# Order of the first loads and of the last products in a convolution and sign-matrix kernel

## The reference

```python
y = conv1d(x, weight, groups=4, K=9, pad=4) + (cond @ c_weight.T)[:, :, None] + bias
w = kernel.astype(float) * 2 - 1          # 1024 x 1024, every entry +1 or -1
out = x + scale * (y @ w)                 # along the 1024 positions
```

## Time and profile before

| | us |
|---|---|
| median of 3 runs | 175.43 (174.07 to 176.49) |
| the profiled execution | 174.09 |
| its span, first to last instruction | 172.2 |
| TensorE matmul busy | 164.2 (95%) |
| VectorE busy | 136.9 (79%) |
| ScalarE busy | 71.8 (42%) |
| GpSimd busy | 37.6 (22%) |
| mean granted TensorE clock | 0.990 |

### The profile page before, as it was taken

One profiled execution on the slowest core, in us unless ns is written; L12 is line 12 of the kernel. 1 busy time (PEld: TensorE's weight loads), 2 busy tenths in 40 slices (PEclk: granted clock), 3 DMA queues, 4 the chain that ended last, 5 costly groups with the idle time before them and its releaser, 6 DMA issues.

```text
span 172.2 us, 2765 instructions
## 1 busy us (share of the span) xinstructions
PE 164.2 (95%) x914; PEld 136.6 (79%) x914; DVE 136.9 (79%) x180; ACT 71.8 (42%) x68; POOL 37.6 (22%) x43
## 2 busy tenths in 40 slices
PE   7699999999999999999999999999999999999791
PEld 2378888998888779887998889887988899888580
DVE  4735493996999999779986899779977997699461
ACT  3201996470791148521781069304842340214000
POOL 4230600005040334006400343043400540000000
PEclk9969999999999999999999999999999999999999
DMA  5688697777799877887977888988888666414006
GB/s 205 139 159 248 249 196 196 125 200 188 143 337 237 256 153 306 184 229 189 297 185 176 262 173 306 225 249 112 331 214 204 94 249 138 105 49 199 0 0 244
DMA packets 27486, 33.38 MB, mean 194 GB/s; under 512 B 3537, under 2 KB 19857, under 8 KB 27473
## 3 DMA queue, kind: packets, MB, share of 16 engines
q1 hardware_dynamic: 22176, 25.63, 54.6%
q10 hardware_dynamic: 4912, 6.78, 14.8%
q0 software_dynamic: 384, 0.81, 2.2%
HBM read 10.06 MB, written 8.40 MB: 107 GB/s over the span
## 4 chain that ended last, share of the span: by engine, by line
PE 92%; DMA 3%; DVE 2%; issue 1%; ACTq 1%; DVEq 0%
PE ps_A L828 30%; PE ps_conv L809 18%; PE ps_C L828 15%; PE ps_conv L786 9%; PE ps_B L828 8%; DMA taps_nat<-weight 3%; PE ps_B L845 2%; PE ps_C L845 2%; PE ps_toep L845 2%; PE ps_A L845 2%; PE ps_toep L828 1%; PE ps_toep L765 1%; PE ps_C L776 1%; PE ps_A L753 1%; DVE sums L250 1%
## 5 line engine op out<-in xcount | busy, mean ns | idle before, releaser
L485 ACT CAST hi<-sums 128x1024 fp32r<-128x1024 f32 x14 | 14.7, 1049 | 44.5 <-DVE sums L622 38.4
L401 POOL TENSOR_TENSOR set<-x_blk 128x512 f32<-128x512 f32 x12 | 17.3, 1461 | 69.7 <-DMA x_blk<-x_phase 69.7
L643 DVE SCALAR_TENSOR_TENSOR x_nat<-ps_A,scale_col,x_nat 128x512 f32<-128x512 f32 x27 | 20.2, 748 | 15.0 <-PE ps_A L828 14.2
L442 ACT COPY x_phase<-x_nat 128x1032 f32<-128x1032 f32 x13 | 27.2, 2135 | 2.2 <-DMA x_nat<-x 2.2
L828 PE MATMUL ps_A<-sign_T,hi 128*128 128x512 f32 x80 | 22.4, 401 | 0.9 <-DVE x_nat L643 0.9
L485 ACT CAST hi<-y_sum 128x1024 fp32r<-128x1024 f32 (+1 forms) x14 | 11.7, 834 | 25.8 <-DMA y_sum<-y_two 16.5
L828 PE MATMUL ps_A<-sign_T,lo 128*128 128x512 f32 x80 | 22.0, 396 | 0.0
L828 PEld LDWEIGHTS ps_A<-sign_T,lo 128*128 128x128 f32 x80 | 15.0, 188 | 3.8 <-DVE lo L632 0.3
L828 PEld LDWEIGHTS ps_A<-sign_T,hi 128*128 128x128 f32 x80 | 14.5, 189 | 4.2 <-issue 1.3
L809 PE MATMUL ps_conv<-toeplitz,w_bytes 128*128 128x128 f32 x144 | 17.2, 276 | 0.4 <-DVE y_two L596 0.4
L809 PEld LDWEIGHTS ps_conv<-toeplitz,set 128*128 128x128 f32 x144 | 16.9, 192 | 0.8 <-issue 0.4
(11 more groups left out here) (108 smaller groups left out, 234.6 us busy)
## 6 DMA issues: line engine op xcount, KB each, us to landing
x_nat<-x SPq DMA_DIRECT2D x16, 512.0 KB, 4.4
out<-x_nat SPq DMA_DIRECT2D x15, 512.0 KB, 4.8
x_blk<-x_phase SPq DMA_DIRECT2D x118, 64.5 KB, 3.0
y_sum<-y_two ACTq DMA_DIRECT2D x48, 128.0 KB, 3.3
w_bytes<-w_bool SPq DMA_DIRECT2D x2, 512.0 KB, 6.5
shift<-shift_dram POOLq DMA_DIRECT2D x2, 256.0 KB, 4.2
x_blk<-x_phase ACTq DMA_DIRECT2D x6, 64.5 KB, 3.7
x_blk<-x_phase POOLq DMA_DIRECT2D x4, 64.5 KB, 3.0
```

The source lines that it names most:

```text
L401: nc.gpsimd.tensor_tensor(dif[r][:, e], x_blk[r][:, :, e:e + M:2], x_blk[r][:, :, e + 1:e + 1 + M:2][:, :, 0:K], ALU.subtract).then_inc(di ...
L442: nc.scalar.copy(x_phase[r][:, :, 0:M + 1], line(d, r, 0, PAD + L + PAD).rearrange("r (m q) -> r q m", q=B)).then_inc(phase_ok[r], B)
L485: nc.scalar.copy(parts(hi_all, k), group(k)).then_inc(hi_ok[k], 1)
L643: nc.vector.scalar_tensor_tensor(there, bank[b], scale2_col[:, :], there, ALU.mult, ALU.add).then_inc(summed[k], 1)
```

## The change

The taps are loaded first on ScalarE's queue. The first half of the sign bytes is sent right behind the first two images on SP's queue. On TensorE 14 matmuls on zeros stand in front instead of 10, the transposes of the taps come ahead of those of the condition, and the context product moves behind the first block of the first convolution, the early shift behind the first block of its second half. Each block of double 0 has its own semaphore and is awaited singly, in the order of `FIRST_ORDER`; the queues share the blocks out differently. The four blocks of the second half of pair (1, 0) are sent from GpSimd's queue. ScalarE makes B21 and B22 ahead of the high part of A12, each in one piece. In the last double P3 stands ahead of P7, and VectorE's sums follow: the low part of S3 and S4, C22_C, C12_A, C12_C, C22_A.

```diff
-WARM = 10, 2
+WARM = 14, 2
-FIRST_BLOCKS = {("SP", 0): (0, 1), ("ACT", 0): (2,), ("POOL", 0): (3,), ("SP", 1): (4,), ("ACT", 1): (5, 6),
-                ("POOL", 1): (7,)}
+FIRST_BLOCKS = {("ACT", 0): (2, 3), ("SP", 0): (0, 1), ("POOL", 1): (4, 5), ("SP", 1): (6,), ("ACT", 1): (7,)}
+FIRST_ORDER = (2, 0, 3, 1), (4, 6, 5, 7)
...
@@ wait_blocks
             if d == 0:
-                for (of, half), blocks in FIRST_BLOCKS.items():
-                    if half == h:
-                        eng.wait_ge(blk_first[r][of, h], 16 * len(blocks))
+                for a in FIRST_ORDER[h]:
+                    eng.wait_ge(blk_first[r][a], 16)
+            elif (d, r, h) == (1, 0, 1):
+                eng.wait_ge(blk_early, 16 * GROUPS)
             else:
-                eng.wait_ge(blk_in[r][h], 16 * GROUPS * d)
+                eng.wait_ge(blk_in[r][h], 16 * GROUPS * (d - 1 if (r, h) == (0, 1) else d))
...
@@ sync
             load(0, 1, x_first[1])
+            signs_in(sp, 0)
             first_blocks(sp, "SP", 0)
             first_blocks(sp, "SP", 1)
-            signs_in(sp, 0)
             load(1, 0, x_first[2])
             signs_in(sp, 1)
             load(1, 1, x_first[3])
-            to_blocks(1, 0)
+            sp.wait_ge(conv_done[0], 2)
+            sp.wait_ge(phase_ok[0], 2 * B)
+            for a in range(GROUPS):
+                to_block(sp, 0, a, blk_in[0][0])
             load(2, 0, x_in[0])
...
@@ gpsimd, behind its copy of the phases of (1, 0)
+            pool.wait_ge(conv_done[0], 2)
+            pool.wait_ge(phase_ok[0], 2 * B)
+            for a in range(GROUPS, NG):
+                to_block(pool, 0, a, blk_early)
             pool.wait_ge(shift_out, 16)
...
@@ scalar
+            act.dma_start(taps_nat[:, :, :], weight).then_inc(taps_in, 16)
             act.dma_start(cond_nat[:, :], cond).then_inc(small_in, 16)
             act.dma_start(cw_nat[:, :], c_weight).then_inc(small_in, 16)
-            act.dma_start(taps_nat[:, :, :], weight).then_inc(taps_in, 16)
...
+                act.wait_ge(w_in[0], 16)
+                sign("B21")
+                sign("B22")
                 high_0("A12")
-                act.wait_ge(w_in[0], 16)
-                sign("B21", KH)
-                sign("B22", 1)
                 high_0("A22")
...
@@ vector
-            dve.wait_ge(small_done, 2)
-            nc.vector.tensor_copy(cond_t[:, :], ps_cond).then_inc(small_ok, 1)
-            nc.vector.tensor_copy(cw_t[:, :], ps_cw).then_inc(small_ok, 1)
             dve.wait_ge(x_first[1], 16)
...
             toeplitz_of(nc.vector.tensor_copy, 1).then_inc(toep_ok, 1)
+            dve.wait_ge(small_done, 2)
+            nc.vector.tensor_copy(cond_t[:, :], ps_cond).then_inc(small_ok, 1)
+            nc.vector.tensor_copy(cw_t[:, :], ps_cw).then_inc(small_ok, 1)
...
-                sum_up("C12_A", d)
-                low_part("S34", d)
...
                 if last(d):
+                    low_part("S34", d)
+                    for k in ("C22_C", "C12_A", "C12_C", "C22_A"):
+                        sum_up(k, d)
                     finish_last(d)
...
@@ tensor
             pe.wait_ge(ident_ok, 1)
-            pe.wait_ge(small_in, 32)
-            nc.tensor.transpose(ps_cond, cond_nat[:, :], ident[0:N, 0:N]).then_inc(small_done, 1)
-            nc.tensor.transpose(ps_cw, cw_nat[:, :], ident[:, :]).then_inc(small_done, 1)
             pe.wait_ge(exp_ok, 2)
...
-            pe.wait_ge(small_ok, 2)
-            nc.tensor.matmul(ps_ctx, cond_t[:, :], cw_t[:, :], start=True, stop=True).then_inc(ctx_done, 1)
+            pe.wait_ge(small_in, 32)
+            nc.tensor.transpose(ps_cond, cond_nat[:, :], ident[0:N, 0:N]).then_inc(small_done, 1)
+            nc.tensor.transpose(ps_cw, cw_nat[:, :], ident[:, :]).then_inc(small_done, 1)
             keep_busy(WARM[1])
+
+            def contexts():
+
+                pe.wait_ge(small_ok, 2)
+                nc.tensor.matmul(ps_ctx, cond_t[:, :], cw_t[:, :], start=True, stop=True).then_inc(ctx_done, 1)
...
@@ conv
+                    for a in FIRST_ORDER[h]:
+                        g = a - h * GROUPS
+                        if d == 0:
+                            pe.wait_ge(blk_first[r][a], 16)
                         for s in range(2):
...
+                        if (d, r, h, a) == (0, 0, 0, FIRST_ORDER[0][0]):
+                            contexts()
+                        if (d, r, h, a) == (0, 0, 1, FIRST_ORDER[1][0]):
+                            early_shift()
...
@@ step
                 if last(d):
                     product("P5", d, bank["C"], True, False, "C12_C")
+                    product("P6", d, bank["A"], False, False, "C11_P1", 1)
+                    product("P3", d, bank["C"], False, True, "C22_C", 1)
+                    product("P7", d, bank["A"], False, False, "C12_A", 1)
```

More of the change, by code:

```diff
@@ L165, in conv_product_kernel @@
         x_in = [sem(f"x_in{s}") for s in range(2)]
-        blk_first = [{(of, h): sem(f"blk_first{r}_{of}{h}") for of, h in FIRST_BLOCKS} for r in range(2)]
+        blk_first = [[sem(f"blk_first{r}_{a}") for a in range(NG)] for r in range(2)]
         blk_in = [[sem(f"blk_in{s}_{h}") for h in range(2)] for s in range(2)]
+        blk_early = sem("blk_early")
         y_in = [sem(f"y_in{s}") for s in range(2)]
@@ L237, in first_blocks @@
             for h in range(2):
-                for a in FIRST_BLOCKS[of, h]:
-                    to_block(eng, r, a, blk_first[r][of, h])
+                for a in FIRST_BLOCKS.get((of, h), ()):
+                    to_block(eng, r, a, blk_first[r][a])
         def first_phases(copy, q):
@@ L422, in _, with sign @@
             first_blocks(act, "ACT", 1)
-            def sign(k, pieces):
+            def sign(k):
                 rows = 0 if k[1] == "2" else KH
                 f = int(k[2]) - 1
[L428 to L432, removed]
+                nc.scalar.activation(signs[k][:, :, :], w_bytes[:, rows:rows + KH, f * BANK:(f + 1) * BANK],
+                                     ACT.Copy, bias=-0.5, scale=1.0).then_inc(sign_ok[k], KH)
             def to_phases(d, r):
@@ L511, in first_double @@
                 act.wait_ge(w_in[1], 16)
-                sign("B11", 1)
+                sign("B11")
                 to_phases(1, 1)
-                sign("B12", 1)
+                sign("B12")
                 high_0("A21")
@@ L729, in step @@
                     last_signs(slice(0, KH // 2))
-                sum_up("C12_A", d)
-                low_part("S34", d)
[L732 to L735, removed]
                 if last(d):
+                    low_part("S34", d)
+                    for k in ("C22_C", "C12_A", "C12_C", "C22_A"):
+                        sum_up(k, d)
                     finish_last(d)
                 else:
+                    sum_up("C12_A", d)
+                    low_part("S34", d)
+                    if d == 1:
+                        last_signs(slice(KH // 2, KH))
+                    sum_up("C22_C", d)
+                    sum_up("C22_A", d)
                     low_part("A", d + 1)
@@ L779, in conv @@
             def conv(d, r):
-                for i in range(2):
-                    wait_blocks(pe, d, r, i)
+                for h in range(2):
+                    if d > 0:
+                        wait_blocks(pe, d, r, h)
                     if r == 1 or d > 0:
-                        pe.wait_ge(y_ok, 8 * d + 4 * r + 2 * i - 2)
-                    for g in range(GROUPS):
+                        pe.wait_ge(y_ok, 8 * d + 4 * r + 2 * h - 2)
+                    for a in FIRST_ORDER[h]:
+                        g = a - h * GROUPS
+                        if d == 0:
+                            pe.wait_ge(blk_first[r][a], 16)
                         for s in range(2):
-                            now = nc.tensor.matmul(ps_conv[:, i, g].rearrange("m u o -> m (u o)"),
-                                                   x_blk[r][:, 2 * g + i, s:s + M],
+                            now = nc.tensor.matmul(ps_conv[:, h, g].rearrange("m u o -> m (u o)"),
+                                                   x_blk[r][:, 2 * g + h, s:s + M],
                                                    toeplitz[:, s, g].rearrange("r u o -> r (u o)"),
                                                    start=(s == 0), stop=(s == 1))
+                        if (d, r, h, a) == (0, 0, 0, FIRST_ORDER[0][0]):
+                            contexts()
+                        if (d, r, h, a) == (0, 0, 1, FIRST_ORDER[1][0]):
+                            early_shift()
                     now.then_inc(conv_done[r], 1)
-                    if (d, r, i) == (0, 0, 0):
-                        early_shift()
             def fast_conv(d, r):
@@ L837, in first_double @@
                     pe.wait_ge(hi_0[of], 1)
+                    pe.wait_ge(sign_ok[k], KH)
                     opens = n < 4
@@ L842, in first_double @@
                         for u in range(KH):
-                            if part is hi:
```

(12 more changed lines are left out.)

1 line of the change is left out of this document (removed).

## The result

The changed kernel takes 170.6 us in the median (170.11 to 171.38, six runs) against 174.79 (174.07 to 176.49, six runs): ratio 0.9748, 95% interval 0.9718 to 0.9778, 4.4 us or 2.5% faster. Its profiled execution took 170.11 us with a span of 168.3, against 174.09 and 172.2. Its own executions still lie 1.27 us apart, with mean granted clocks of 0.998 to 1.000. The ratios of the experiments leave out every execution that is over 1.5% above the fastest of its kernel: one with 10 warm matmuls, one with 14 in the kernel before, one with the taps third, and four of ten with the taps first in the kernel before (176.8 to 180.4 us).

What follows compares the result with a forecast made beforehand. TensorE, busy 95% of the span, was taken as the bound, with only idle or slow stretches recoverable. 174.09 - 2.6 (start) - 1.3 (end) = 170.2, or 171.5 from the median; 170.8 was taken, range 169.1 to 173.6.

Steps and rivals of the forecast that it cites:

- the head: Start-up through double 0's convolutions: they end near 17.0 against 19.54, gaining 2.6 us; bounds 3.0 and a loss of 1.0.
- the tail: Last double to the end: new product order and earlier even-image store gain 1.3 us, bounds 0.8 and 1.8.
- From 170.2 to 170.8: Whole kernel: 170.2 from the profiled execution, 171.5 from the other runs' median; 170.8 taken between, if TensorE's slow stretch differs.
- Taps first and warm-up: Start: taps land at 3.5 instead of 6.13, expansion 1.1 us earlier, transposes at 6.4, clock 1.00 through the convolutions.
- The far end of 7.3: Start: end of the warm matmuls if four more cost 1.75 us instead of 0.87; an end of the range, 0.9 us.
- Signs ahead of y: First products: signs made by 14.5, high and low part of A12 by 15.9 against 17.0; cost nothing, up to 1.1.
- the first half ends at 10.5: First convolution: last block lands about 10.0, plus 4 x 0.116, so its first half ends at 10.5 rather than 12.94.
- P3 ahead of P7: Last double: P3 starts with no wait, P7's sum is done beside it; TensorE gains 1.31, last piece 1.2 us earlier.
- The landing term: End of the kernel: final stores land sooner once the even image's 512 KB store leaves 3 us earlier; tail's upper bound 1.8.
- A: First convolutions: clock falls all the same behind TensorE's holes, costing 1.5 us, time 172.3; chance 0.20.
- B: Start: sign bytes hold the taps until 8.6, head loses 2.5 us, time 175.3 to 176.6; chance 0.08.
- C: First convolutions: SP's blocks start behind the sign bytes and come 1.0 later, time 171.8 to 172.3; chance 0.17.

Runs made afterwards that it cites:

- both of the last edits: Changed kernel with P6 of double 1 between the fast convolutions of double 2, and the early shift directly behind the first half: ratio 0.9804.
- the two other traces with its start: Kernel before with only the last double's new order, ratio 0.9855; the same with SP's store of the even image held for the sum behind P7, 0.9905.
- P6 between: Changed kernel with P6 of double 1 placed between the two fast convolutions of double 2: ratio 0.9832.

## Why the prediction was right, by its steps

The forecast was 170.8, range 169.1 to 173.6; measured 170.6. The direction, the whole and the likeliest case held. That the whole is met so closely is in part luck: by the traces the head gave 0.7 us less than its forecast and the tail 0.6 more, and the two errors cancel.

*From 170.2 to 170.8:* the step between the profiled execution and the median supposed that executions differ by the slow stretch of TensorE. They do not in the main: the changed kernel has no such stretch and its executions still differ by 1.27 us, and those of the kernel before with the full clock are not its fastest. What makes them differ stays open.

*Taps first and warm-up:* right in place. Transposes from 6.52 (forecast 6.4), clock 1.00 throughout, warm matmuls ending at 6.2 (forecast 6.4). The far end of 7.3 came too, in the trace with both of the last edits, and moved the convolutions' end only to 18.29; there all fourteen matmuls took 0.44 us each. I had taken the clock row of 1.00 as the sign that the added ones would take half of that, and in this trace the row reads 1.00 all the same. But the full clock was worth nothing by itself: 14 warm matmuls in the kernel before gained nothing.

*Signs ahead of y:* forecast at no cost, which holds (the high part of A12 was done at 15.77, 2.4 us before its product). Its worth was forecast at nothing too, and there the step failed. I looked at what the moved signs might delay and not at when the old signs would have become due: bytes at 17, ScalarE until 21, against convolutions that now end at 18. Undone, it costs 2.6 us.

*Head, 2.6 us:* by the runs 2.6 (1.8 to 3.4), by the traces 1.4 at the end of the convolutions and 1.9 in the span, since they end at 18.17 and not near 17.0. The step that failed is "the first half ends at 10.5". I took the last block's landing as the end and left out TensorE's own work before it: from 8.78 the five blocks and the context product run without a gap until 11.67, which puts the first half's end near 11.2. The forecast's own rows would have said so: 64 instructions at 0.116 and the shift's 1.05 from 8.5 on end at 17.0 with no wait at all. So 2.6 was the best case and not the middle, and the bound of 3.0 could not be reached. The start itself was 0.3 late, since its first block landed at 8.64, and the wait of 0.3 for VectorE's first sum stood in no step. What comes on top of 1.4 comes later in the traces (the second fast convolution starts 1.83 us earlier than before) and from the trace it is compared with: the profiled execution of the kernel before was its fastest of six, and the two other traces with its start end the convolutions at 20.00 and 21.02.

*Blocks awaited singly:* 0.8 us, no separate term in the forecast.

*P3 ahead of P7:* TensorE's 1.31 and the last sum's 1.2 held (1.31 measured between P6 and the last sum). The landing term was mis-sized: 0.1 forecast, 0.5 as its far end, 0.6 to 0.8 in the traces, since the store of the even image was out of the queue. Tail forecast 1.3, in the traces 1.9, by the runs 2.5 (1.9 to 3.2).

*Rivals.* A did not come to pass (mean clock 0.998 and more in all six executions), but it stood close: with four warm matmuls fewer the clock fell, for 1.5 us as priced. B names a mechanism that is there: with the sign bytes early the third small load takes 5.3 us to land instead of 4.5, but in first place the taps take 3.7 with the bytes and without. Where B did come about, with the taps third, they landed at 7.44 and not 8.6, and the convolutions ended 3.3 us later than before, more than B's 2.5, since the half clock now lasted until 15. C did not show: TensorE had no wait for a block after its first.

## What to carry to other kernels

Ask of each moved transfer not only what it delays but when its old place would have become the bound once everything else is faster: here the warm matmuls and the early taps are worth nothing alone (0.9992, 0.9988) and 1.5 and 4.9 us when taken out of the whole. This start-up is a race of several chains that end together, and it had to be changed together. The small load that all else waited for goes first on its queue. And where a product is moved in front of a wait, follow the other engine's written order: VectorE here had no slack to give.

## What the runs showed of the hardware

**GpSimd's DMA issues beside VectorE's copies.** In the kernel before a block issue of GpSimd took 0.53 us. In the changed kernel the first took 2.02, from 5.51 to 7.53, and VectorE's fp32 copies run from 5.11 to 7.42; with the taps third VectorE idles there, and two issues take 1.06. First the changed kernel, then that one:

```profile
5.51 2.02 POOL L233 DMA_DIRECT2D x_blk<-x_phase  x1 [2.01 <-ACT x_phase L245]
```

```profile
5.49 1.06 POOL L233 DMA_DIRECT2D x_blk<-x_phase  x2 [1.98 <-ACT x_phase L245]
```

The Trainium skill (SBUF — State Buffer, section "SBUF: two separate sides") says that GpSimd can't write its descriptors while VectorE's fp32 copies hold the ports that the two share. The times here agree: the issue ends 0.11 us behind the copies. It cost nothing this time, by a little: the block landed at 10.8 and TensorE came to it at about 11.2.

**VectorE beside GpSimd's arithmetic.** A VectorE fp32 instruction (`sums`, 128x512) of 0.68 us took up to 1.56 while GpSimd's two ran beside it; which of VectorE's instructions are hit depends on a shift of a microsecond.

**Small loads beside large ones.** The taps, third on ScalarE's queue, landed 4.2 to 4.7 us after issue with 1 MB on SP's queue (four traces) and 5.7 with 1.5 MB. First on the queue they took 3.6 to 3.7 in every trace, with 1 MB or 1.5 MB. The Trainium skill (DMA: Bandwidth & Descriptors, "Queues, rings and completion order") has each DMA engine go round robin between queues, packet by packet, by which 36 KB should hardly wait; the measurement decides here, and why the small loads waited stays open.

**Warm-up.** Fourteen warm matmuls in front took 4.99 us in the changed kernel's trace, 6.10 in the one with both edits and, in the one with P6 between,

```profile
1.19 5.69 PE ps_A L761 x14
```

though nothing is changed at the start. In the trace with both edits all fourteen take 0.44 us each; in the changed kernel's the last five or so take half of that (an estimate from the 4.99). The granted clock reads 1.00 from the first microsecond on in both, so at the very start that row says nothing of the rise, which is read from the durations. It does not stand at a fixed distance from the first matmul. The Trainium skill (TensorE: Matmul & The Clock Gate, Part 1) says the same of it: it comes some half a microsecond earlier or later from run to run.
